# A key projection and half a query projection written as two passes of 64-row tiles around the second logits

## What is computed

```
q = (layernorm(x) @ Wq).reshape(b, n, 32, 16)
k, v = split(ctx @ Wkv)                     # ctx has 256 columns
q, k = apply_axial_rope(q, pos), apply_axial_rope(k, pos)
w = softmax(einsum('bqhd,bkhd->bhqk', q, k) / 4)
x = x + tanh(g_xattn) * (einsum('bhqk,bkhd->bqhd', w, v) @ Wout + bout)
h = square(relu(f @ up_w))                  # f = layernorm(x)
y = h @ down_w + (f @ expert_weight) * (sum of the two largest f @ gate_w)
x = x + tanh(g_ffn) * layernorm(y) * ln_gamma + ln_beta terms
```

## Time and profile before

| | us |
|---|---|
| median of 3 runs (1567.04 to 1567.78) | 1567.08 |
| the profiled execution | 1566.75 |
| its span, first to last instruction | 1564.9 |
| PE busy with matmuls | 1515.9 |
| DVE busy | 980.2 |
| ACT busy | 635.0 |

### The profile page before, as it was taken

One profiled execution on the slowest core, in us unless ns is written; L12 is line 12 of the kernel. 1 busy time (PEld: TensorE's weight loads), 2 busy tenths in 40 slices (PEclk: granted clock), 3 DMA queues, 4 the chain that ended last, 5 costly groups with the idle time before them and its releaser, 6 DMA issues.

```text
span 1564.9 us, 25920 instructions
## 1 busy us (share of the span) xinstructions
PE 1515.9 (97%) x9498; PEld 1125.0 (72%) x9498; DVE 980.2 (63%) x1416; ACT 635.0 (41%) x962; POOL 337.9 (22%) x406
## 2 busy tenths in 40 slices
PE   7789999999999999979999999999999999999997
PEld 6556666666666666646787888878888888788886
DVE  7788888888888888755655436435354264453524
ACT  4365665655555666665432222222222222222221
POOL 5323233333333333112101002001020020110202
PEclk9699999999999999999999999999999999999999
DMA  6645555555555555544411001101011010010101
GB/s 174 142 98 141 134 137 138 131 142 139 135 135 143 127 127 136 121 134 120 147 61 35 27 21 47 35 15 47 21 35 47 1 54 27 22 40 21 55 0 41
DMA packets 80623, 131.11 MB, mean 84 GB/s; under 512 B 21624, under 2 KB 35064, under 8 KB 80504
## 3 DMA queue, kind: packets, MB, share of 16 engines
q1 hardware_dynamic: 80504, 129.48, 32.4%
HBM read 51.17 MB, written 16.78 MB: 43 GB/s over the span
## 4 chain that ended last, share of the span: by engine, by line
PE 88%; DVE 7%; issue 2%; POOL 1%; ACT 1%; DMA 0%; SPq 0%; POOLq 0%; DVEq 0%; ACTq 0%
PE pP L1113 17%; PE pT L1113 11%; PE pA L1314 11%; PE pO L1113 11%; PE pB L1314 11%; PE pA L1211 7%; PE pO L1239 7%; PE pB L1227 3%; PE pM L1113 3%; DVE mneg L1534 3%; PE pP L1120 2%; PE pM L1120 2%; PE pT L1195 1%; PE pM L1281 1%; PE pM L1187 1%
## 5 line engine op out<-in xcount | busy, mean ns | idle before, releaser
L1534 DVE TENSOR_REDUCE mneg<-pA 128x4 f32<-128x1024 f32 x250 | 305.7, 1223 | 97.7 <-PE pA L1211 93.2
L1012 ACT ACTIVATE probs<-pB 128x1024 f32<-128x1024 f32 x249 | 255.8, 1027 | 213.2 <-PE pB L1227 203.3
L811 POOL TENSOR_SCALAR var_eps<-meanvar 128x1 f32<-128x1 f32 x96 | 34.6, 360 | 986.1 <-DVE meanvar L1416 985.9
L1637 DVE TENSOR_TENSOR relu<-relu 128x512 f32<-128x512 f32 x128 | 88.4, 690 | 252.3 <-ACT hid L1066 252.3
L1314 PE MATMUL pA<-dn,hid 128*128 128x512 f32 x768 | 197.1, 392 | 1.7 <-DVE hid L1639 1.5
L1314 PE MATMUL pB<-dn,hid 128*128 128x512 f32 x768 | 195.0, 389 | 0.0
L1113 PE MATMUL pP<-fT,up 128*128 128x512 f32 x768 | 188.5, 394 | 0.0
L1113 PE MATMUL pO<-fT,up 128*128 128x512 f32 x768 | 184.7, 389 | 0.0
L1314 PEld LDWEIGHTS pA<-dn,hid 128*128 128x128 f32 x768 | 142.9, 188 | 34.4 <-DVE hid L1639 5.1
L1113 PEld LDWEIGHTS pO<-fT,up 128*128 128x128 f32 x768 | 144.0, 188 | 30.3 <-issue 0.4
L1314 PEld LDWEIGHTS pB<-dn,hid 128*128 128x128 f32 x768 | 144.1, 188 | 30.0
(11 more groups left out here) (200 smaller groups left out, 1989.8 us busy)
## 6 DMA issues: line engine op xcount, KB each, us to landing
stk<-kT SPq DMA_DIRECT2D x180, 128.0 KB, 2.9
stq<-qT SPq DMA_DIRECT2D x180, 128.0 KB, 2.9
fres<-x_scratch SPq DMA_DIRECT2D x34, 256.0 KB, 2.9
xin<-x SPq DMA_DIRECT2D x32, 256.0 KB, 2.9
numer<-av_s SPq DMA_DIRECT2D x128, 64.0 KB, 2.4
xres<-x SPq DMA_DIRECT2D x32, 256.0 KB, 2.9
x_scratch<-xres SPq DMA_DIRECT2D x32, 256.0 KB, 2.4
out<-y_s SPq DMA_DIRECT2D x32, 256.0 KB, 2.0
```

The lines of the kernel that those rows point to most:

```text
L811: nc.gpsimd.tensor_scalar_add(var_eps[:], meanvar[:, 1:2], EPS).then_inc(ve_made, 1)
L1012: nc.scalar.activation(probs[:, s % 4, :, :, :].rearrange("p a b s -> p a (b s)"), psum[:, :, :], ACT.Exp).then_inc(exp_done, 1)
L1534: nc.vector.tensor_reduce(mneg[par][:, :, 2 * u:2 * u + 2].rearrange("p t q -> p q t"), psum[:, :, :].rearrange("p q (t k) -> p q t k", t= ...
L1637: nc.vector.tensor_tensor(r[:], r[:], r[:], ALU.mult).then_inc(sq_made, 1)
```

## The change

In step 7 of the iterations 0 to 13, `K1` and `Q1<` are no longer two runs of six matmuls of 128 rows. Each 128-row matmul becomes two of 64 rows, and the work is written in two passes. In the first pass the lower 64 rows (0 to 63) of each of the six `K1` matmuls alternate with the upper 64 rows of the six of `Q1<`: twelve matmuls, in pairs that use different halves of the array and different banks. The second pass has the halves swapped. The first pass stands between the first and the second logits of step 7, the second pass behind the second logits. Both banks are now asked for ahead of the first pass, so ahead of the second logits, and the second pass waits for the end of the first (`rows_done`). The accumulation in a bank goes on over both passes, in pP also over step 8, whose half stays as it is.

```diff
+PAIRS = {7: ("K1", "Q1<")}
...
+            def paired(names, i, s, par, swapped):
...
+                if swapped:
+                    pe.wait_ge(rows_done, pair_number(i, s))
+                sides = []
+                for k, name in enumerate(names):
+                    half, name = (0, name[:-1]) if name[-1] == "<" else (None, name)
+                    b, at, bank = i + LAG[name], (par + LAG[name]) % 2, BANK[name]
+                    if not swapped:
+                        if some(number(name, b) - 1):
+                            pe.wait_ge(taken[bank], number(name, b) - 1)
+                        inputs_of(name, b, half)
+                    rows = slice(HALF_ROWS, P) if (k == 1) != swapped else slice(0, HALF_ROWS)
+                    sides.append(({"P": pP, "M": pM, "T": pT}[bank], rows, half, bank) + factors(name, b, at))
+                for c in range(CC):
+                    for a, w in PASSES:
+                        opens = not swapped and c == 0 and (a, w) == PASSES[0]
+                        closes = swapped and c == CC - 1 and (a, w) == PASSES[-1]
+                        for psum, rows, half, bank, lhs, rhs, _ in sides:
+                            last = nc.tensor.matmul(psum[:, :], lhs(a, c)[rows, :], rhs(w, c)[rows, :],
+                                                    start=opens, stop=closes and half is None)
+                            if closes and half is None:
+                                last.then_inc(done[bank], 1)
+                if not swapped:
+                    last.then_inc(rows_done, 1)
...
+                    pair = pair_at(i, s)
+                    if pair:
+                        paired(pair, i, s, par, False)
                     if within(i):
                         logits_b(i, par % 2, s)
...
+                    if pair:
+                        paired(pair, i, s, par, True)
                     for name in names_at(i, s):
-                        job(name, i, par)
+                        if name not in pair:
+                            job(name, i, par)
```

More of the change, by code:

```diff
@@ L141, in first_maxima, with pair_at, pair_number @@
     return isinstance(b, int) and b == 0 and u < STEPS - DELAY
+def pair_at(i, s):
+    names = PAIRS.get(s, ()) if within(i) else ()
+    return names if all(live(x.rstrip("<"), i) for x in names) else ()
+def pair_number(i, s):
+    return sum(bool(pair_at(j, t)) for j in range(i + 1) for t in PAIRS if (j, t) <= (i, s))
 def before(names, i):
@@ L154, in number @@
     names = [x for x in ORDER[BANK[name]] if not two_step or x in TWO_STEP]
+    if isinstance(i, int) and i == -1:
+        names.sort(key=lambda x: x[0] != "V")
     return before(names, i) + sum(live(x, i) for x in names[:names.index(name) + 1])
@@ L359, in flamingo_gated @@
         f_lo = sem("f_lo")
+        rows_done = sem("rows_done")
         o_done = sem("o_done")
@@ L1160, in opening, with inputs_of, factors @@
                 pe.wait_ge(o_taken, len(OPENING))
+            def inputs_of(name, b, half):
+                if name[0] == "K":
+                    pe.wait_ge(ctx_split, 2 * b + 2)
+                elif name[0] == "O":
+                    pe.wait_ge(at_lo, 2 * b + (1 if half == 0 else 2))
+            def factors(name, b, par):
+                cut = slice(int(name[-1]) * P, (int(name[-1]) + 1) * P)
+                if name[0] == "Q":
+                    return lambda a, c: xnT[a][:, c, :], lambda w, c: wq_s[w][:, c, :], KC
+                if name[0] == "O":
+                    return (lambda a, c: rest(b, c // 2)[:, c % 2, cut] if a else aT_hi[:, c, cut],
+                            lambda w, c: wo_s[w][:, c, :], KC)
+                weights = wk_s if name[0] == "K" else wv_s
+                return (lambda a, c: ctx_s[par][a][:, c, cut], lambda w, c: weights[w][:, c, :], CC)
@@ L1166, in compute @@
                     last = turn(psum, lambda c: xn[:, c * P:(c + 1) * P])
[L1167 to L1179, removed]
+                elif name[0] in "QKVO":
+                    inputs_of(name, b, half)
+                    last = product(psum, *factors(name, b, par), half)
                 elif name[0] in "qk":
```

## The result

The changed kernel takes 1576.36 us (median of 4 runs, 1575.32 to 1577.99) where the kernel before takes 1567.06 (median of 4 runs, 1566.80 to 1567.78); the ratio is 1.006, with a 95% interval of 1.0042 to 1.0077. The profiled execution has a span of 1573.7 us, 8.8 more than before.

What follows compares the result with a forecast made beforehand. PE's own sequence was taken to bound the kernel (idle 0.15 of 42.09 us). Per iteration 3.71 us becomes 4.36, + 0.65, 14 times + 9.1; on the profiled 1566.75 that gives 1575.9, plus 0.33 for the median: 1576.2 us, range 1571 to 1584.

Steps and rivals of the forecast that it cites:

- That the wait for pP is the loss, and where it ends: Step 7, ahead of the first pass: PE waits for DVE to free pP, opening a 0.85 us hole plus 0.10 load.
- That the pairs run side by side at full rate, with their loads hidden: Both passes in step 7: each 512-column pair takes 0.23 us, adding nothing; upper end 0.24, + 0.12 an iteration.
- The rival with loads that show in each pair: Both passes in step 7: each pair exposes a 0.10 us load, + 16.8 us, 1593.0; chance 0.05, shared with slower pairs.
- the one with a lower rate: Both passes in step 7: a pair takes 0.30 us, not 0.23, giving 1588.0; within the 0.05 chance of exposed loads.
- the one with pairs whose matmuls run one after the other: Both passes in step 7: no overlap within pairs, + 38.6 us, 1614.8; chance 0.01.
- That the changes of form go: First logits of step 7 to step 8: both switches between 64-row tiles and 128 rows vanish, saving 0.37 us an iteration.
- the rival that 48 or 50 rows and 64 rows are different forms: Between passes and logits: nothing saved, two switches of row form added, + 10.4 us, 1586.6; chance 0.05.
- The hole between the passes: Step 7: second pass waits for the first's end; 0.31 us less 0.24 covered by second logits leaves 0.07; range 0 to 0.30.
- The count for the late exponential: ACT's step 7 exponential, delayed, still frees pB before step 8's second logits need it, with 0.3 us to spare.
- The sum for each iteration: First logits of step 7 to step 8's first matmul: 3.71 us becomes 4.36, + 0.65 in each of 14 iterations.
- That behind iteration 13 all runs relative to PE and DVE: After the changed iterations, the rest of the program shifts with PE and DVE, so the whole + 9.1 us remains.
- The other side: Step 7: pP freed by T (first logits' start) + 0.3 saves 0.30 us an iteration, 1562.9; break-even T + 0.5; chance 0.03.

Runs made afterwards that it cites:

- the wait alone: Kernel before the change plus only a PE wait for pP ahead of step 7's second logits, no tiles: 1579.38 us, 1.0083 of the kernel before.
- the wait moved forward: Changed kernel with X1 ahead of kT0 in step 5 and kT0 in bank pT, so pP is freed earlier: 1568.53 us, 1.0012 of the kernel before.
- the needless matmul: Kernel before the change plus an unneeded 256-column matmul between step 7's first and second logits: 1573.36 us with 128 rows, 1567.33 with 64.

## Why the prediction was right, and where its terms were off

The forecast was 1576.2 us, the measured median is 1576.36. That is nearer than the working deserves: the loss of an iteration was put 0.12 us too low, which is 1.7 us over fourteen, and the end of the program came 2.1 us less late than the iterations do. The two nearly cancel, and that is luck.

- **That the wait for pP is the loss, and where it ends**: right in kind, shown by the wait alone and by the wait moved forward. The release came as read, at T + 1.13. The first pass was forecast at T + 1.19 and began at T + 1.28: from the end of DVE's instruction to the first load it is 0.12 here, where 0.05 had been taken from the maxima. It is 0.12 too with both passes behind the logits and with the wait moved forward. With the wait alone it was 0.06 (338.82 to 338.88). The instruction behind which PE stands has waits for three semaphores in the kernels with the pair and two with the wait alone; whether that is the reason was not tested. The idle time in the row is 0.78, not the 0.85 to 0.95 that was to be seen, since the row counts from the modelled end of the logits (T + 0.50) and the forecast from T + 0.34.
- **That the pairs run side by side at full rate, with their loads hidden**: right. A pair every 0.23, with two loads of 0.18 in it. The rival with loads that show in each pair (1593.0) and the one with a lower rate (1588.0) are out. So is the one with pairs whose matmuls run one after the other (1614.8). The rule of the Trainium skill ("TensorE: Matmul & The Clock Gate", What overlaps and what doesn't), that a load overlaps running matmuls only where the row group differs, does not hold for this form: the load of `K1`'s lower rows at 337.56 runs under the matmul of the same rows at 337.56, and the next one starts 0.23 later.
- **That the changes of form go**: right. No load waits behind the second pass, so the rival that 48 or 50 rows and 64 rows are different forms (1586.6) is out. Their price was 0.37 by the sum and 0.42 by the needless matmul.
- **The hole between the passes**: forecast 0.07, measured 0.12. The second logits start at 338.72 and stream for 0.24, to 338.96; the second pair of the second pass starts at 339.31, so the first streams from 339.08. The end of the first pass and the load were rightly counted; the 0.05 for the semaphore was 0.06 and the ends in the trace are a little later. The count for the late exponential held: it ends at 339.18 + 1.03 = 340.21, and the second logits of step 8, which need its bank, start at 340.70 (T + 4.73), behind the first ones as ever.
- **The sum for each iteration**: forecast + 0.65, measured + 0.77. The 0.07 at the release and the 0.05 at the hole are the difference. Times 14 that is 10.8 us, and at the end of the iterations the changed kernel is indeed 10.9 us behind (the same logits at 656.29 and at 667.20).
- **That behind iteration 13 all runs relative to PE and DVE**: wrong. The end of the span is only 8.8 behind. In the kernel before and in the changed one:

```profile
656.29 0.51 PE L1211 MATMUL pA<-stk,stq 48*128 48x256 f32 x4
...
668.79 0.76 PE L1195 MATMUL pT<-low 32*128 32x256 f32 x2 [1.96 <-issue]
...
673.62 1.14 PE L1239 MATMUL pO<-probs,v 128*17 128x256 f32 x16
...
1553.79 1.52 PE L1314 MATMUL pB<-dn,hid 128*128 128x512 f32 x6
```
```profile
667.20 0.50 PE L1261 MATMUL pA<-stk,stq 48*128 48x256 f32 x4
...
678.77 0.76 PE L1245 MATMUL pT<-low 32*128 32x256 f32 x2 [1.03 <-issue]
...
683.61 1.91 PE L1289 MATMUL pO<-probs,v 128*17 128x256 f32 x16
...
1563.44 1.52 PE L1370 MATMUL pB<-dn,hid 128*128 128x512 f32 x6
```

At the second row, the spread of the reciprocals, PE waited 1.03 us instead of 1.96, and the distance shrinks from 10.9 to 10.0. But that is no lasting gain. From these waits on the granted clock is at its lower level, 1.2 GHz, for some 7 us in either kernel. The sixteen matmuls of the third row fall into that stretch in the changed kernel and for the most part behind it in the kernel before. Windows of both, before and after (columns as in the earlier trace rows, the granted clock third from the end):

```profile
673.62:674.69 1.07, 1.07 (x18) 0.36 (x16) 0.91 (x1) 0.96 (x1) 1.01 (x1) 0.89 0.24 54
683.61:685.44 1.83, 1.83 (x18) 0.49 (x16) 0.91 (x1) 1.02 (x1) 1.28 (x1) 0.51 0.17 28
```

They take 1.91 us instead of 1.14, and the distance is 10.8 again. The prediction looked at the clock in the iterations alone, where it stays up. So it goes on, up and down with the waits and with stretches of the lower clock, to 9.65 at the last matmuls; and what stands behind them took 8.7 us instead of 9.6. The row names no releaser ("issue"), so what PE waited for there is open. The other kernels show that this part gives as well as takes. By the iterations the wait alone should be 14 x 0.93 = 13.0 behind and is 13.3 at the last matmuls; half the number of pairs 5.4 and is 5.2; both passes behind the logits 10.8 and is 12.8. How much of it varies between runs of one kernel was not looked at, but the four runs of the changed kernel lie 2.7 us apart, those of before 1.0. The steady measure is the repetition.
- **The other side** (the bank free in time, 1562.9) didn't happen in this kernel, but its price was tried: pP freed 0.59 earlier moved the time by 7.8 us. That the break-even is a release at T + 0.5 was too favourable by the same 0.12: at T + 0.54 the repetition was 0.16 above that of before. With banks free at T + 0.42 at another place, tiles and passes gave 0.31 an iteration, 4.3 us over fourteen.

## What to carry over

Writing full-height matmuls as two passes of half-height tiles between other half-height work saves two changes of form, here some 0.4 us a place, but it opens both banks at once and at the earlier of the two places. So ask of the banks first: where does the last instruction that empties them end, compared with the matmul that is to come first? An engine that is level with the matmuls at that place (DVE with two instructions still ahead of it) makes the hoisted wait dearer than the saving; a pair of jobs whose banks are empty earlier gives most of the gain without it (0.31 us), and jobs of neighbouring steps can share a pair, one pass in each.

## What the runs showed of the hardware

Full-height and half-height matmuls were added into one bank's sum in turn, also with another half-height group in between: `Q1` in steps 7 and 8, `O1` in steps 13 to 15. A single half-height matmul ahead of a half-height pair starts together with the pair's first (both at 206.70), so a lone tile costs 0.09 us a time (42.184 - 42.091), less than its 0.12. A wait of PE for its own last matmul costs little: the next load starts 0.06 us behind the matmul's modelled end, and then comes the load's 0.10. In the iterations, with 0.95 us of idle time in each 42.86, the granted clock stays at 2.4 GHz (1.00).
